# Two message-passing layers on one core: dense work ahead of the gathered group's products

## The reference

```
h = max(layernorm(x), 0)
for layer in (1, 2):
    msg = concat(h[src], edge_attr) @ W_msg.T
    agg = segment_sum(msg, dst)             # 12,500 x 128
    h   = gru_cell(agg, h, Wih, Whh, bih, bhh)
out = x + h
```

## Time and profile before

| | |
|---|---|
| Median of the timed runs | 3290.52 us |
| The profiled execution | 3279.4 us, span 3277.7 us |
| PE matmul busy | 2630.1 us (80% of the span), weight loads 2360.7 us |
| POOL busy | 2324.6 us (71%) |
| DVE busy | 1530.0 us (47%) |
| ACT busy | 999.1 us (30%) |
| TensorE clock granted, mean | 0.835 of full |

### The profile page before, as it was taken

One profiled execution on the slowest core, in us unless ns is written; L12 is line 12 of the kernel. 1 busy time (PEld: TensorE's weight loads), 2 busy tenths in 40 slices (PEclk: granted clock), 3 DMA queues, 4 the chain that ended last, 5 costly groups with the idle time before them and its releaser, 6 DMA issues.

```text
span 3277.7 us, 74395 instructions
## 1 busy us (share of the span) xinstructions
PE 2630.1 (80%) x20375; PEld 2360.7 (72%) x20376; DVE 1530.0 (47%) x4895; ACT 999.1 (30%) x2343; POOL 2324.6 (71%) x2389
## 2 busy tenths in 40 slices
PE   0689889899898898898975777787787787787887
PEld 0578778788787787787855676687677677686675
DVE  5544455454454544545443444444444445444444
ACT  5212223232232333332341222232232233333333
POOL 4477777777777776776717777777777777777772
PEclk9988798798798898988986777777787787887888
DMA  7233333333333333333315222222222222222221
GB/s 195 56 88 86 86 94 90 85 94 88 87 93 88 85 91 82 92 80 80 88 33 128 54 55 58 56 62 55 61 59 58 60 63 60 64 60 62 65 61 43
DMA packets 350922, 249.44 MB, mean 76 GB/s; under 512 B 226506, under 2 KB 312334, under 8 KB 350628
## 3 DMA queue, kind: packets, MB, share of 16 engines
q0 software_dynamic: 75232, 155.02, 17.5%
q1 hardware_dynamic: 254617, 70.47, 10.3%
q10 hardware_dynamic: 20779, 20.48, 2.1%
HBM read 226.51 MB, written 19.20 MB: 75 GB/s over the span
## 4 chain that ended last, share of the span: by engine, by line
PE 35%; POOL 30%; issue 16%; DVE 6%; DVEq 4%; DMA 3%; ACT 3%; ACTq 1%; SPq 1%; POOLq 1%
POOL rows L666 30%; PE ps_v L762 9%; PE ps_win L802 8%; PE ps_win L786 4%; PE ps_q L755 3%; DVEq L1187 2%; PE ps_c L755 2%; PE ps_b L879 1%; PE ps_b L880 1%; PE ps_d L866 1%; PE ps_d L895 1%; ACT hr L1366 1%; PE ps_a L886 1%; DVEq L1217 1%; PE ps_c L888 1%
## 5 line engine op out<-in xcount | busy, mean ns | idle before, releaser
L666 POOL DMA_INDIRECT rows<-h_table,idx x1156 | 1153.2, 998 | 485.3 <-issue 376.2
L666 POOL DMA_INDIRECT rows<-x_table,idx x1156 | 1144.5, 990 | 410.4 <-issue 402.1
L802 PE MATMUL ps_win<-onehot,rows 128*128 128x80 f32 x4624 | 743.3, 312 | 202.5 <-DMA rows<-x_table,idx 162.8
L802 PEld LDWEIGHTS ps_win<-onehot,rows 128*128 128x128 f32 x4624 | 663.7, 221 | 248.7 <-issue 145.9
L762 PE MATMUL ps_v<-hr,a_blk 125*128 125x128 f32 x4800 | 715.2, 319 | 0.0
L762 PEld LDWEIGHTS ps_v<-hr,a_blk 125*128 125x128 f32 x4800 | 698.4, 235 | 0.8
L1385 ACT COPY a_blk<-ps_q 125x224 f32<-125x224 f32 (+5 forms) x504 | 223.8, 480 | 856.3 <-PE ps_q L755 763.7
L1115 DVE SCALAR_TENSOR_TENSOR v_hot<-v_cur,lane 128x42 bf16<-128x42 f32 (+13 forms) x1180 | 435.1, 425 | 0.0
L786 PE MATMUL ps_win<-onehot,attr 128*64 128x80 f32 x3128 | 312.2, 253 | 120.2 <-DVE onehot L1130 80.4
L755 PE MATMUL ps_q<-v_hot,lo_hot 128*125 128x28 bf16 (+5 forms) x3696 | 289.4, 222 | 139.9 <-DVE v_hot L1115 117.7
L755 PEld LDWEIGHTS ps_q<-v_hot,lo_hot 128*125 128x125 bf16 x3696 | 272.5, 151 | 151.2 <-DVE v_hot L1115 128.9
(11 more groups left out here) (191 smaller groups left out, 2038.3 us busy)
## 6 DMA issues: line engine op xcount, KB each, us to landing
attr<-in_edge_attr_dram SPq DMA_DIRECT2D x390, 128.0 KB
rows<-h_table,idx POOLq DMA_INDIRECT x1156
rows<-x_table,idx POOLq DMA_INDIRECT x1156
dst_in<-in_dst_dram SPq DMA_DIRECT2D x678, 2.0 KB
idx<-in_src_dram SPq DMA_DIRECT2D x576, 2.0 KB
x_table<-out_sb ACTq DMA_DIRECT2D x50, 125.0 KB
attr<-in_x_dram ACTq DMA_DIRECT2D x50, 125.0 KB
out_dram<-out_sb ACTq DMA_DIRECT2D x50, 125.0 KB
```

The lines of the kernel that those rows point to most:

```text
L666: nc.gpsimd.indirect_dma_start(out=rows[0:parts, s, j, :], out_offset=None, in_=table[:, :], in_offset=bass.IndirectOffsetOnAxis(ap=idx[0: ...
L802: mm = nc.tensor.matmul(ps_win[r % 2][:, 0:WIN], rows[0:parts, rr, j, :], onehot[0:parts, r % 2, j, :], start=(j == 0), stop=(j == TILES - 1))
```

## The change

In each place PE does the dense work first and the gathered group's products behind it. `window_of_block` at `gi` = 21 moves ahead of that place's group as well. Nothing is added or taken away, and DVE's, ACT's, POOL's and SP's programs stay as they are.

```diff
@@ -904,8 +904,6 @@
                         if gi is None:
                             attr_group(place(layer, it, q), slot(layer, q), attr_n)
                         else:
-                            group(place(layer, it, q), slot(layer, q), gi % RING, P,
-                                  attr_n, gather_use(layer, it, gi))
                             sl, phase = divmod(gi, 3)
                             if gi >= USED:
                                 if gi == USED:
@@ -915,6 +913,8 @@
                                 pack(blk, sl, 2 * phase + 1)
                             else:
                                 slice_multiply(blk, sl)
+                            group(place(layer, it, q), slot(layer, q), gi % RING, P,
+                                  attr_n, gather_use(layer, it, gi))
                         last = q + 1 == len(order(layer))
                         if last or (gi is not None and gi % RING == RING - 1 and gi + 1 < SLOTS):
                             u = SUBS - 1 if last else gi // RING
```

## The result

The changed kernel takes 4067.03 us (median of four runs, 4053.44 to 4073.16) against 3289.86 us: a ratio of 1.2362, 95% interval 1.2342 to 1.2382. It is 777 us slower; the forecast was 3750 us, with 3880 as the end of its range. The profiled execution took 4072.09 us.

A forecast was written before the change was run, and what follows sets the result against it. PE was taken to set the pace from mid layer 0, POOL in layer 1. Stalls and half clock added 353 us in layer 0 and 112 in layer 1 to 3279.4: 3744, called 3750 us, range 3400 to 3880.

The forecast's parts named there:

- A: PE's wait for DVE's v_hot before packs 2 and 3, every slice: 1.9 us in layer 0, 1.8 in layer 1.
- the sum: Forecast's addition of slice and block times: + 353 us in layer 0, + 112 in layer 1, 3744 us in all.
- B: PE's wait for DVE's v_hot before packs 0 and 1, in slices without a chunk: 1.25 us layer 0, 1.8 layer 1.
- Half clock behind B: After the wait before packs 0 and 1, clock falls half the time: 0.1 us on packs, 0.45 on the group.
- half clock nearly throughout: Rival, chance 0.14: B brings half clock in every slice too, 165 us more over 24 blocks, about 3900 us.
- The block's end: Last multiplication of a block to the next block's first, with one chunk: 42.5 us layer 0, 27.6 layer 1.
- the allowance of 2 us for other stalls: Term in a layer 1 block without a chunk: 2 us for other stalls, within its 120 us.
- There is none before a block's first packs: At a block's start: no B before its first packs, because they follow groups 21 to 23.
- Layer 1's slices: Forecast time of a slice in layer 1: 16.3 us without a chunk, 18.5 with one.
- POOL's pace: One gather in 1.296 us, 124 us a block, three groups 15.5; said to bound layer 1 and leave PE slack.
- Other queues: POOL's gathers and SP's loads wait for later PE releases, 5 us for POOL; said to be covered or lose nothing.
- The case of stalls without clock: Rival, chance 0.14: the stalls come but the clock falls no more often than now, about 3420 us.

## Why the prediction was wrong

- **The direction, the mechanism and the length of the stalls were right, but for A behind a chunk.** In slices without a chunk A was 1.9 and 1.80 us in the sum and is 1.87 and 1.69 on average; B was 1.25 and 1.8 and is 1.17 and 1.82. The waits for `v_hot` come to 543.9 us, where 400 to 500 were named. DVE's order is the cause: with it turned round, 745 of 777 us go. A chunk does cover B, but A behind it is longer, 2.4 us in layer 0 and 2.7 in layer 1, where the sum kept 1.9 and 1.8. Why it is longer there has no run of its own. In layer 1, behind a chunk:

```profile
3454.14 0.94 PE L755 MATMUL ps_q<-v_hot,lo_hot 128*125 128x28 bf16 x14
...
3458.90 0.65 PE L755 MATMUL ps_q<-v_hot,lo_hot 128*125 128x56 bf16 x8 [2.59 <-DVE v_hot L1115]
```

- **Half clock behind B was sized wrong, too low in layer 0.** The step that failed is "Stall B, at 1.25 us, I take to do so half the time". In the trace after, 44 of 52 PE gaps of 1.0 to 1.4 us that began at full clock are followed by half clock within 3 us of their end; in the kernel before it was 10 of 21, which is where "half" came near. A begins 3 to 5 us after B's end with no multiplication between, and the clock does not come back between the two. The slices without a chunk show it: the group behind B and the packs and group behind A were 2.1 + 1.3 + 2.6 us in the sum and are 2.8 + 1.7 + 3.0 in the trace, since A now begins at half clock, where the sum let the clock fall a microsecond into the packs. The whole step is 1.65 us over in 43 slices, 71 us. Filling B alone gave 60 us. The multiplication itself was right (5.0 us). The chunk slices of layer 0, which have no B, are 1.4 us over, 35 us; the longer A is 0.5 of it. The rival "half clock nearly throughout" was right on the group behind B in layer 0 (3.05 against 2.8 measured), wrong on its packs (2.12 against 1.3) and on layer 1, and its 3900 us were short too.
- **The block's end was the larger miss.** The sum built it from parts: 42.5 us in layer 0 (its block of 143.8 less six slices of 17.75, plus 5.2 for a chunk) and 27.6 in layer 1, worked out in the same way. It is 48.7 and 40.6. Over the eleven ends, each with its own chunks, that is 67 and 139 us. Two things were wrong. The parts did not give the kernel before: there the end already took 41.3 and 35.8 us, 24.6 and 22.1 of them at half clock, and a comparison with the trace would have shown in layer 1 that the allowance of 2 us for other stalls stood against 12.7 us of idle time. And the change itself adds 7.4 and 4.8 us, by waits for which the sum has no term (of new stalls there it says only "There is none before a block's first packs"): `lo_hot` and `v_hot` of the next block, 3.9 us of DVE, are made behind group 20, the multiplication used to cover them, and now groups 22, 23 and the chunk wait. Restoring the two slices brings the end back to 40.2 and 35.9.
- **Layer 1's slices** were 1.2 us too high without a chunk (16.3, measured 15.1) and 1.4 too low with one. That takes 52 us off and puts 35 on. Of the 1.2 us, 0.8 are the packs and group behind B: 1.5 + 1.75 in the sum and 1.2 + 1.2 in the trace, as most of both is done before the clock falls. Of the 1.4 us, 0.9 are the longer A behind a chunk. The two slice terms of layer 1 nearly cancel, which is luck.
- **The account.** 71 + 35 + 9 (two chunks) + 67 in layer 0 and -52 + 35 + 8 + 139 in layer 1 is 312 us; the profiled execution lies 328 above the 3744 of the sum. Two thirds of it are the block's ends.
- **POOL's pace** was right as a mean of a block and wrong as a picture of a slice. In the kernel before a slice without a chunk takes 12.2 us, less than three groups of POOL (15.5), since POOL gets ahead during the 36 to 41 us at a block's end: its lead over PE, in groups gathered and not yet multiplied, falls in layer 0 from 3.5 at a block's first multiplication to 2.2 at its last. So slices of both layers had less slack than the prediction saw. That the loss per slice reached the time nearly in full for this reason fits, but has no run of its own.
- **Other queues** were no cause, as forecast: POOL waits 695 us for PE's products, and PE waits for rows only once.
- **The case of stalls without clock** (3420 us) is excluded: the mean clock fell to 0.737, and filling the stalls with work makes the kernel 364 us faster.
- How far the clock's 427 us of busy time split between A, B and the shorter waits was not measured one by one. That packs 0 and 1 ahead cost 314 us on top of the moved multiplication, above what I had worked out, stays without its own test.

## What to carry to other kernels

Before moving work on one engine, list for each wait behind it what the moved work was covering, on every engine, also where the consumer is not the next instruction; here two of three covers were seen and the third, at the loop's seam, was not. Build the kernel before from the same parts as the kernel after and compare it with the trace, stretch by stretch: a term that misses there misses in the forecast. When the order of a consumer changes, the producer's order has to change with it: here packs first costs 1.2% in place of 23.6% once DVE builds their `v_hot` first.

## What the runs showed of the hardware

- Waits of about a microsecond can cost the clock, and sometimes shorter ones do. Of PE's waits of 1.0 to 1.4 us in the kernel after, 44 of 52 were followed by half clock within 3 us; of those of 0.6 to 1.0 us it was 54 of 169 with the multiplication moved alone, but 1 of 26 in the kernel after. Moving the multiplication alone put 0.76 us in front of it; slices without a chunk in layer 0 grew by 1.9 us, of which 1.0 is idle time, and have 0.8 us more at half clock.
- Busy work alone did not bring full clock back here. In the kernel after, 168 of 193 stretches at half clock ended while a multiplication (28 or 30 products of 125x128) ran and the other 25 in a chunk's products; none ended in packs or in a group's products. In the kernel before, PE was busy with those from 376.2 to 389.0 us without a break and stayed at half clock.
- Idle time of PE costs more than its length: 3384 spare matmuls in the waits took 364 us off the changed kernel (mean clock 0.737 to 0.846). It depends on the place: 20 of them before the last attribute group of the kernel before gave nothing (0.9999).
- Five register loads on DVE in a row held it for 3.3 us: the 3.28 us without an instruction are gone from that place once the loads are moved. Out of the chain that PE waits for, they were worth 0.7% of this kernel.
